# Rotary embedding from one projection by halves, and the order of work between a mixture-of-experts layer and attention

## The reference, cut to what matters

```python
x = L0_attn_x                                   # (4, 1024, 128)
x = x + 0.5 * ffn(layernorm(x), Wr, W1, W2)     # 8 experts, top 2 of them weighted
x = x + attn(layernorm(x), qkv_w, qkv_b, out_w, out_b)
x = x + 0.5 * ffn(layernorm(x), Wr, W1, W2)

def apply_rotary(x):                            # x: (B, 16 heads, T, 8)
    x1, x2 = (x[..., ::2], x[..., 1::2])
    return concatenate([x1 * cos - x2 * sin, x2 * cos + x1 * sin], axis=-1)
```

## Time and profile before

| | us |
|---|---|
| median of 3 runs | 1300.66 |
| lowest, highest | 1300.22, 1306.47 |
| the profiled execution | 1300.45 |
| its span, first to last instruction | 1298.7 |
| first layer of experts, last PE work at | 352.5 |
| from there until attention runs at full clock | 352.5 to 392 |
| attention | 392 to 998 |
| second layer of experts | 998 to 1298.7 |
| PE's steps in the chain: `hidden` of an expert, `expert_out` | 2.59, 1.79 |
| a store to `k_stack`, from issue to landing, median | 2.3 |

### The profile page before, as it was taken

How to read it: one execution, slowest core, us unless ns; L and a number is a source line. 1 busy time by engine, 2 the same in 40 slices (tenths; PEclk the granted TensorE clock), 3 DMA queues, 4 the chain that set the end, 5 groups by cost and what they waited for, 6 DMA issues and landing times.

```text
span 1298.7 us, 32041 instructions
## 1 busy us (share of the span) xinstructions
PE 1258.2 (97%) x10240; PEld 613.8 (47%) x10240; DVE 1107.9 (85%) x2306; ACT 807.2 (62%) x1540; POOL 141.7 (11%) x450
## 2 busy tenths in 40 slices
PE   5999999999979999999999999999999999999998
PEld 3666666667622222222222222222223777767776
DVE  7888867887789999999999999999994778777775
ACT  4433333333229999999999999999997333323332
POOL 1020122111221111111111111111110000000000
PEclk9999999999969999999999999999999999999999
DMA  7010111011211111111101011011111000100000
GB/s 211 1 31 19 50 50 41 8 49 50 68 55 33 33 41 31 37 35 31 41 31 41 31 33 39 31 41 31 40 47 32 19 28 28 28 27 25 9 10 9
DMA packets 52265, 48.49 MB, mean 37 GB/s; under 512 B 10080, under 2 KB 44768, under 8 KB 52192
## 3 DMA queue, kind: packets, MB, share of 16 engines
q1 hardware_dynamic: 52192, 47.61, 12.6%
HBM read 23.86 MB, written 23.33 MB: 36 GB/s over the span
## 4 chain that ended last, share of the span: by engine, by line
PE 63%; DVE 29%; issue 7%; DVEq 1%; ACT 0%; DMA 0%; SPq 0%; ACTq 0%
DVE mx L1257 25%; PE ps L780 23%; PE ps L767 16%; PE ps L922 8%; PE ps L909 7%; PE ps L880 2%; PE ps L737 2%; PE ps L757 1%; DVE X L1114 1%; PE ps L701 1%; PE ps L744 1%; DVE act L1102 1%; PE ps L774 1%; DMA w<-w_t 0%; PE ps L719 0%
## 5 line engine op out<-in xcount | busy, mean ns | idle before, releaser
L1257 DVE TENSOR_REDUCE mx<-ps 128x1 f32<-128x1024 f32 x512 | 587.3, 1216 | 22.3 <-PE ps L880 20.9
L676 ACT ACTIVATE probs<-ps 128x512 f32<-128x512 f32 x1024 | 557.3, 601 | 41.9 <-PE ps L909 33.9
L605 ACT ACTIVATE sg<-ps,unscale 128x512 f32<-128x512 f32 x256 | 173.8, 687 | 306.7 <-PE ps L780 285.1
L880 PE MATMUL ps<-K,Q 48*128 48x512 bf16 x1008 | 321.9, 388 | 7.1 <-DVE mx L1257 3.4
L922 PE MATMUL ps<-probs,vh 128*32 128x256 f32 x4096 | 327.8, 392 | 0.0
L909 PE MATMUL ps<-Q,K 51*128 51x512 bf16 x1024 | 319.0, 384 | 0.9 <-ACT probs L676 0.7
L767 PEld LDWEIGHTS ps<-w,act 128*128 128x128 f32 x2048 | 247.9, 192 | 17.1
L767 PE MATMUL ps<-w,act 128*128 128x128 f32 x2048 | 249.0, 275 | 0.0
L1102 DVE SCALAR_TENSOR_TENSOR act<-ps,unscale,sg 128x512 f32<-128x512 f32 x256 | 183.5, 745 | 58.1 <-PE ps L780 18.2
L780 PE MATMUL ps<-x_hi,w_hi 128*128 128x512 f16 x512 | 194.8, 381 | 10.1 <-DVE act L1102 6.2
L1114 DVE SCALAR_TENSOR_TENSOR X<-ps,rw,X 128x128 f32<-128x128 f32 (+1 forms) x512 | 144.0, 344 | 61.7 <-PE ps L767 61.2
(11 more groups left out here) (84 smaller groups left out, 607.9 us busy)
## 6 DMA issues: line engine op xcount, KB each, us to landing
o_parts<-ot SPq DMA_DIRECT2D x64, 128.0 KB, 1.9
q_stack<-parts SPq DMA_DIRECT2D x48, 128.0 KB, 2.3
k_stack<-parts SPq DMA_DIRECT2D x48, 128.0 KB, 2.3
Q<-q_stack SPq DMA_DIRECT2D x64, 96.0 KB, 2.3
K<-k_stack SPq DMA_DIRECT2D x64, 96.0 KB, 2.3
probs<-w_in SPq DMA_DIRECT2D x8, 256.0 KB, 4.7
att<-o_parts SPq DMA_DIRECT2D x16, 128.0 KB, 2.6
rden<-rdens SPq DMA_DIRECT2D x16, 128.0 KB, 2.5
```

What stands on the lines that cost most here:

```text
L605: nc.scalar.activation(sg[:, j, :], hid[2 * j], ACT.Silu, scale=unscale[:, e, 2 + j:3 + j]).then_inc(silu_done, 1)
L676: nc.scalar.activation(probs[:, kb % PSLOTS, j * CH:(j + 1) * CH], score[u][i], ACT.Exp, scale=SCALE).then_inc(probs_ready, 1)
L880: last = nc.tensor.matmul(maxps[t % 2][:, half, :], Q[u][0:STACK, t * P:(t + 1) * P], K[u][0:STACK, half * CH:(half + 1) * CH], start=True ...
L1257: nc.vector.tensor_reduce(mx[:, u % 2, t:t + 1], pair.rearrange("p a b -> p (a b)"), AX_X, ALU.max).then_inc(max_read, 1)
```

## The change

- **One projection.** The columns of the q and k weights are put in the order "first members of all pairs, then second members", 64 and 64. `q_or_k` is one product of 128 x 512, q into `mpsum_all`, k into `tpsum`, and k no longer waits for the rotation of q. `rotate` is three DVE instructions: all 128 rows times `cos`, and twice 64 rows times `sin`, written to the other 64 rows of `rot`. Weights, bias and tables follow; the packed weights shrink from five to three matrices.
- **Stores.** The parts of a chunk lie on the partitions by halves, so each store becomes two, of 64 partitions: 12 DMAs for q and 12 for k, of half the bytes.
- **First heads.** Heads 0 to 2 are loaded when the stores of chunks 0 to 5 have landed, ahead of the stores of chunk 6.
- **First maximum.** Tiles 0 and 1 of head 0 stand among the last experts of chunk 7: tile 0 behind `hidden` of expert 7, tile 1 behind `expert_out` of expert 6. The other six stand as before.
- **The row of the maxima.** On POOL the maxima of head 0 are split before the second and third step of k's last parts; PE transposes them after 4 instead of 7 of head 1's products; ACT copies them before the middle part of k; SP sends them between the stores of q and of k of chunk 7.
- **Bias.** `add_bias` of chunk 7 moves from ahead of head 1's maxima to behind the last maximum of attention, ahead of `norm_attention(0, 0)`.

```diff
-            for w in range(2):
-                sp.wait_ge(stored[w], 16 * GROUPS * (NCH - 1))
...
                     for g, i in enumerate(which):
-                        dst = stack[bass.ds(r * H, H), g * HD:(g + 1) * HD, u * CH:(u + 1) * CH]
-                        sp.dma_start(dst, parts[:, w, i, :]).then_inc(stored[w], 16)
+                        for a in range(2):
+                            row = g * HD + a * HD // 2
+                            dst = stack[bass.ds(r * H, H), row:row + HD // 2, u * CH:(u + 1) * CH]
+                            sp.dma_start(dst, parts[a * HALF:(a + 1) * HALF, w, i, :]).then_inc(stored[w], 16)
...
+            for w in range(2):
+                sp.wait_ge(stored[w], STORED * (NCH - 2))
+            sp.wait_ge(stacks_ready, 1)
+            for u in range(3):
+                load_head(0, u)
             store_parts(NCH // CPB - 1, 0)
...
-            store_parts(NCH // CPB - 1, 1)
+            store_parts(NCH // CPB - 1, 1, only=(0,))
             load_mrow(0, 0)
+            store_parts(NCH // CPB - 1, 1, only=(1,))
...
+            qk_sum(last_chunk, 0)
+            qk_rest(last_chunk, 0)
+            qk_lo(last_chunk, 0)
+            qk_sum(last_chunk, 1)
+            max_parts(0, 0)
+            qk_rest(last_chunk, 1)
+            qk_lo(last_chunk, 1)
             pool.wait_ge(v_ready, NCH)
...
-            for w in range(2):
-                hi_part(NCH - 1, w)
-                mid_part(NCH - 1, w)
+            hi_part(NCH - 1, 0)
+            mid_part(NCH - 1, 0)
+            hi_part(NCH - 1, 1)
...
             mrow_copy(0, 0, 0)
+            mid_part(NCH - 1, 1)
...
-                if w:
-                    pe.wait_ge(rot_ready, 2 * c + 1)
-                else:
+                if not w:
                     at_least(pe, route_ready, c)
-                for i, bank in enumerate((mpsum_all, tpsum)):
-                    last = nc.tensor.matmul(bank, wqkv[:, 2 * w + i, :], x2T[:], start=True, stop=True)
-                last.then_inc(qk_in_psum, 1)
+                nc.tensor.matmul(qk_bank[w], wqkv[:, w, :], x2T[:], start=True, stop=True).then_inc(qk_in_psum, 1)
...
+            def first_max_scores(t):
+                if t < 2:
+                    pe.wait_ge(silu_done, 2 * E * NCH - 1 + t)
+                    pe.wait_ge(act_ready, 2 * E * NCH - 1 + t)
+                    pe.wait_ge(head_loaded[0], 32)
+                elif t == 2:
+                    pe.wait_ge(acc_done, E * NCH)
...
+                    if maxes and e == E - 1:
+                        first_max_scores(0)
...
+                if not attended:
+                    first_max_scores(1)
                 expert_out(E * (p0 + NCH) - 1, E - 1)
...
-                if i == MT_AT:
+                if i == FIRST_MT_AT:
                     max_transpose(0, 0, 0, first=True)
...
-                for i, (bank, table) in enumerate(((mpsum_all, cos), (tpsum, sin))):
-                    last = nc.vector.scalar_tensor_tensor(out=rot[:, w, i, :], in0=bank,
-                                                          scalar=bqk[:, 2 * w + i:2 * w + i + 1],
-                                                          in1=table[:, at], op0=ALU.add, op1=ALU.mult)
+                nc.vector.scalar_tensor_tensor(out=rot[:, w, 0, :], in0=qk_bank[w], scalar=bqk[:, w:w + 1],
+                                               in1=cos[:, at], op0=ALU.add, op1=ALU.mult)
+                for half in range(2):
+                    src, dst = slice(half * HALF, (half + 1) * HALF), slice((1 - half) * HALF, (2 - half) * HALF)
+                    last = nc.vector.scalar_tensor_tensor(out=rot[dst, w, 1, :], in0=qk_bank[w][src, :],
+                                                          scalar=bqk[src, w:w + 1], in1=sin[src, at],
+                                                          op0=ALU.add, op1=ALU.mult)
                 last.then_inc(rot_ready, 1)
...
             keep_values(last_chunk, B - 1, 1)
-            add_bias(last_chunk)
-            dve.wait_ge(bias_added, NCH)
...
+            add_bias(last_chunk)
+            dve.wait_ge(bias_added, NCH)
             norm_attention(0, 0)
```

More of the change, by code:

```diff
@@ L71 @@
 FIRST_PAIRS = 3
+FIRST_MT_AT = 4
 W_OPS = 5
@@ L368, in load_head @@
                                  stack[bass.ds(n, 1)].rearrange("n s t -> (n s) t")).then_inc(head_loaded[u], 16)
+            for u in range(CPB):
+                store_parts(0, u)
+            with sp.Fori(1, NCH // CPB - 1) as r:
+                for u in range(CPB):
+                    store_parts(r, u)
+            for w in range(2):
[3 more added lines that the diff above has]
+                load_head(0, u)
+            store_parts(NCH // CPB - 1, 0)
             def load_mrow(r, u):
@@ L781, in hidden, with ffn_chunk @@
                 return last
-            def ffn_chunk(p, k, first, more, back, proj, loads):
+            def first_max_scores(t):
[5 more added lines that the diff above has]
+                    pe.wait_ge(acc_done, E * NCH)
+                at_least(pe, max_read, t - FIRST_PAIRS + 1)
+                for j in range(2):
+                    last = nc.tensor.matmul(first_maxps[t % FIRST_PAIRS][:, j, :], Q[0][0:STACK, t * P:(t + 1) * P],
+                                            K[0][0:STACK, j * CH:(j + 1) * CH], start=True, stop=True)
+                last.then_inc(max_in_psum, 1)
+            def ffn_chunk(p, k, first, more, back, proj, loads, maxes=False):
                 done = 0 if back is None else back + 1
@@ L821, in ffn, with chunk @@
             def ffn(p0, attended):
-                def chunk(c, u, first=False, more=True, loads=False):
+                def chunk(c, u, first=False, more=True, loads=False, maxes=False):
                     back = None if attended or first else c - 1
-                    ffn_chunk(p0 + c, u, first, more, back, c + 1 if attended and more else None, loads)
+                    ffn_chunk(p0 + c, u, first, more, back, c + 1 if attended and more else None, loads, maxes)
                 if not attended:
@@ L837, in ffn @@
                 chunk(NCH - 2, 0)
-                chunk(NCH - 1, 1, more=False)
+                chunk(NCH - 1, 1, more=False, maxes=not attended)
+                if not attended:
+                    first_max_scores(1)
                 expert_out(E * (p0 + NCH) - 1, E - 1)
@@ L1230, in ffn @@
                 ffn_chunk(p0, rounds - 1, 0, ahead=False)
-                ffn_chunk(p0, rounds - 1, 1, more=False, ahead=False)
+                ffn_chunk(p0, rounds - 1, 1, more=False, ahead=False, maxes=p0 == 0)
+                if p0 == 0:
+                    first_max(1)
                 accumulate(E * (p0 + NCH) - 1, E - 1, NCH - 1, 1)
```

112 lines of the change are left out of this document (57 added, 55 removed).

## The result

The changed kernel takes 1296.82 us, median of 10 runs (1292.59 to 1298.04). The kernel before, run ten times beside it, takes 1303.99 (1300.21 to 1306.47). The ratio is 0.9945, 95% interval 0.9930 to 0.9961: faster by 0.55%. The forecast was 1288.0 with a range to 1292.5, so it had the sign and not the size. Executions of the kernel before fall in two groups, near 1301 and near 1306 us, and the profiled one (1300.45) is of the first group; the changed kernel's profiled one took 1295.86, so the sum is checked on their difference, -4.6 (predicted -12.5), where the medians differ by 7.2.

What follows compares the result with a forecast made beforehand. It took PE, with DVE not far behind, to bound the experts, and DVE's order and PE's half clock the passage. Chunks -12.04 and passage -0.5 gave -12.5 from 1300.45, forecast 1288.0 us, range 1285.0 to 1292.5.

Steps and rivals of the forecast that it cites:

- The whole 1.72: Expert chunks: each of seven gains all 1.72 us of its two halved projections, 12.04 in all, DVE keeping up.
- Rival 1: Expert chunks: bias meeting POOL or halves of nearly 1 us take back 2 to 6 us; chance 0.13.
- The rotation: DVE's three-instruction rotation of q or k: some 2.25 us by the partition rule, 1.99 without it.
- Rival 4: DVE rotation: reading and writing different row halves is a slow path, kernel slower, 1322 us; chance 0.03.
- -1.79: Passage to attention: one q product less on PE at half clock saves 1.79 us.
- +1.05: Passage: two maxima tiles moved among the last experts make the normalized chunk ready 1.05 us later.
- +1.84: Passage: two rotations with three instructions each cost DVE 1.84 us more.
- +0.3: Passage: DVE, back before PE at half clock has made head 1's first tile, loses 0.3 us.
- Nothing in the change alters that: Head 0 in attention: PE stays at half clock after 384 until 391 us, DVE waiting, as before.
- SP: Store queue: q's 12 stores take 7.6 us, maxima row leaves at 378.9 instead of 380.29, worth 0.
- Rival 2: SP's 24 DMAs make head 0's row or head 3's load late, 1289.5 to 1291 us; chance 0.10.
- The bias at the end of attention: Last chunk's bias behind the last maximum: 0.9 us plus 0.1 wait, cost 0, or 0.8 if one addition stalls.

Runs made afterwards that it cites:

- the halves alone: Kernel before with only the one-product projections, three-instruction rotation, new tables and halved stores, nothing of the new order: 1305.74 us, ratio 1.0015.

## Why the prediction was wrong

**"The whole 1.72."** This step failed. The walk of the chunk had the right parts: the bias at 214.2 in the old frame (it said 214.4), POOL's last step on q at 214.6, as it said, PE's need at 217.4. It charged one stall of 0.85 and found 0.5 us left. It left out POOL's next instruction, k's sum, which had been ready since the rotation ended and so ran without a gap: two stalls, 2.05 us in all, of which 0.57 reaches PE. POOL's queue was followed for the step in question and not for the one behind it. By the Trainium skill ("SBUF — State Buffer", section "SBUF: two separate sides") a Vector instruction with two SBUF inputs and a GpSimd one shut each other out for a whole instruction; the rows agree, additions of 1.25 and 1.36 us beside steps of 1.16 and 1.32. Price: 3.2 us of the 3.6 in the chunks. Rival 1 named the mechanism at 2 to 6 us and got 0.13, because "it needs both", the meeting and halves of nearly 1 us; the meeting was enough, with halves of 0.75, because the longer rotation put the bias onto two steps.

**The rotation.** Right. A half takes 0.75 us, 0.76 from start to start, so a rotation takes 2.3 us where the sum had 2.25. The Trainium skill's rule on a change of partitions ("VectorE: DVE Perf Modes", section "Two Vector instructions with no wait between them") gave 2.25 as well, and the rows side with it against 1.99: the whole form starts every 0.66. No run has halves that keep to their own rows, so the rule is not told apart from a property of instructions on 64 rows. Rival 4 fell.

**The passage.** -1.79 for the halved product came out as -1.58 (364.63 to 356.03, less 7.02 at the normalized chunk); two tiles at +1.05 were +1.5, which the run without them shows; +1.84 was +2.1; the bias gave 1.6; the +0.3 for head 1's first tile didn't come. With +0.1 for the values the terms behind the normalized chunk add to -1.0, as the table has it, and what came behind that tile was +0.1 instead of -0.2. What the sum did not see is that PE's waits ahead of the transposes are longer after the change, 1.22 + 4.62 where 2.54 (for head 0's load) + 2.39 stood, and that the clock then has no full stretch in the passage: before had one from 364.3 to 371.1 us. The steps were priced at half clock already, so this cost the forecast little, but 2.7 us lay there unseen.

**"Nothing in the change alters that", of the clock.** Said of 384 to 391 us, true there, and never asked of the end of attention. No row of before showed a fall at 985 us, but two waits of 0.18 and 0.52 stood there. The end of attention stood in the sum at 0; it took 3.1 of the 7.9 us between the two profiles. That the copies on ACT cause the longer wait is shown; why the clock falls after it in the changed kernel's profile, and not in before's nor with the halves alone, is open.

**SP.** Right: 12 stores took 7.6 and 8.2 us, the row left 8.4 sooner, PE's first scores started at 375.2 and nobody waited for head 3's load. Rival 2 fell. That the order pays for the stores is what the halves alone show; the text gave the row 0 and didn't say how much that 0 stood on.

**The bias at the end of attention.** Right: 0.88 us, no stall, and PE's `out_projection` at 969.87 without a wait.

## What to carry to other kernels

When an edit lengthens a stretch of one engine, lay the other engines' queues beside the new times and read on past the step that collides: the next one in the queue may be ready and run without a gap. Price the parts of a change each alone as well as together: here the part with all the gain was worth nothing (1.0015) until the order of loads, stores and rows was changed with it. And a wait that costs nothing may still cost the clock: look at PE's gaps and at the granted clock behind them, the long ones first (4.62 us here). Where PE is needed right after a long one, work that nobody reads can pay.

## What the runs showed of the hardware

- Four additions of 128x128 float32 between SBUF tiles take 0.89 us on DVE alone, 2.94 beside two back-to-back steps of POOL of 1.16 and 1.32 us. All 32 additions together take 19.4 us, and 7.1 with the bias at expert 3.
- The half clock outlasts the waits that it followed: in the changed kernel PE's longest wait ended at 351.9 us, from 370 to 380 PE was 9.03 of 10 us busy at 0.50, and full clock came back only at 384.4. With 28 products of 0.22 us in the gaps the clock stayed full through 364.
- A store's issue on SP takes as long for 64 rows as for 128: 0.63 us, and 0.68 to 0.71 for q's in the last chunk.
- Waits of PE of 0.18 and 0.52 us at the end of attention came ahead of half clock (some 6.5 us of it, about 3 us lost) in six profiles and not in three others.
